# Attention scores of one core: a three-part fp32r product becomes one fp32 product

## The reference, cut to what matters

```python
q = (x @ Wq + bq)                      # 8 heads of 128
kv = x @ Wkv + bkv                     # one key and one value head, shared by the 8
k, v = kv[..., :128], kv[..., 128:]
q = q + pe[None, None, :, :]           # sinusoidal positions
k = k + pe[None, :, :]
scores = einsum('bhqd,bkd->bhqk', q, k) / sqrt(128)
scores = where(causal, scores, min)
attn = einsum('bhqk,bkd->bhqd', softmax(scores), v)
out = attn.reshape(B, T, 8 * 128) @ Wo
```

## Time and profile before

| | us |
|---|---|
| median of 3 runs (lowest to highest) | 880.68 (879.22 to 882.73) |
| the profiled execution's own time | 883.31 |
| its span, first to last instruction | 881.5 |
| PE busy | 680.0 (77%) |
| DVE busy | 546.7 (62%) |
| ACT busy | 415.1 (47%) |
| POOL busy | 300.3 (34%) |

### The profile page before, as it was taken

The page is one execution under the profiler, slowest core; times in us unless marked ns, Lnnn a source line. Parts: engine busy times, 40 slices in busy tenths (PEclk is TensorE's granted clock), DMA queues, the critical chain, the costliest instruction groups (busy, mean ns, idle before and its releaser), DMA issues. The chain is left out here.

```text
span 881.5 us, 11690 instructions
## 1 busy us (share of the span) xinstructions
PE 680.0 (77%) x3456; PEld 474.4 (54%) x3468; DVE 546.7 (62%) x820; ACT 415.1 (47%) x824; POOL 300.3 (34%) x211
## 2 busy tenths in 40 slices
PE   4889999999989689999999898501766666675764
PEld 2656666666659566666666654100555555561222
DVE  5264333343323234433445448977999998999998
ACT  1255555555525355455555668422454552553330
POOL 0012122101100022112211100786776763768882
PEclk9589999999979999999999998855699997996998
DMA  9200000000556500000000000113254552440112
GB/s 306 60 3 10 10 9 12 6 3 7 152 156 214 164 10 10 10 9 9 6 3 7 6 1 1 45 39 119 65 153 147 177 156 83 157 142 24 36 33 57
DMA packets 45761, 57.63 MB, mean 65 GB/s; under 512 B 6049, under 2 KB 32418, under 8 KB 45730
## 3 DMA queue, kind: packets, MB, share of 16 engines
q1 hardware_dynamic: 32994, 46.23, 16.8%
q0 software_dynamic: 3072, 6.30, 2.4%
q10 hardware_dynamic: 9664, 4.72, 1.8%
HBM read 43.60 MB, written 13.63 MB: 65 GB/s over the span
## 5 line engine op out<-in xcount | busy, mean ns | idle before, releaser
L437 POOL TENSOR_TENSOR QL<-QF,QH 128x512 fp32r<-128x512 f32 x32 | 40.6, 1268 | 409.4 <-ACT QH L558 409.4
L1353 DVE TENSOR_REDUCE nmax<-PS 128x1 f32<-128x128 f32 (+7 forms) x128 | 96.6, 756 | 116.2 <-PE PS L828 114.7
L566 ACT COPY PT<-PS 128x512 f32<-128x512 f32 (+1 forms) x192 | 85.8, 482 | 139.0 <-PE PS L840 138.9
L856 PE MATMUL PS<-PT,V 128*128 128x512 f32 (+3 forms) x384 | 151.0, 505 | 0.2 <-ACT PT L566 0.2
L482 POOL TENSOR_TENSOR YA<-YA,HC 128x1024 f32<-128x1024 f32 x44 | 103.9, 2362 | 53.9 <-DVE HS L1514 53.3
L815 PE MATMUL PS<-KH,QH 128*128 128x512 f32 (+1 forms) x192 | 87.3, 455 | 19.6 <-POOL QL L437 19.0
L573 ACT ACTIVATE PR<-PS,nmax 128x128 f32<-128x128 f32 (+7 forms) x128 | 96.4, 753 | 5.5 <-DVE nmax L1353 5.5
L840 PE MATMUL PS<-CST,PR 128*128 128x128 f32 x576 | 85.7, 276 | 14.5 <-ACT PR L573 14.4
L840 PEld LDWEIGHTS PS<-CST,PR 128*128 128x128 f32 x576 | 68.4, 142 | 48.7 <-issue 32.1
L1047 PE MATMUL PS<-R,pickb 128*128 128x512 bf16 x58 | 23.0, 482 | 79.8 <-DVE HS L1514 34.7
L1369 DVE SCALAR_TENSOR_TENSOR X<-PS,rinv,X 128x128 f32<-128x128 f32 x128 | 36.1, 345 | 74.1 <-PE PS L878 74.1
(11 more groups left out here) (200 smaller groups left out, 1287.0 us busy)
## 6 DMA issues: line engine op xcount, KB each, us to landing
mw<-in_w SPq DMA_DIRECT2D x40, 512.0 KB, 4.4
mw<-in_w SPq DMA_DIRECT2D x16, 321.0 KB, 4.1
more_w<-in_w SPq DMA_DIRECT2D x16, 321.0 KB, 3.6
rows_in<-zero SPq DMA_DIRECT2D x18, 256.0 KB, 3.5
MX<-rows_in SPq DMA_DIRECT2D x20, 128.0 KB, 4.2
rows_out<-MY ACTq DMA_DIRECT2D x20, 128.0 KB, 2.8
rows_out<-MY ACTq DMA_DIRECT2D x8, 256.0 KB, 4.3
X<-in_x SPq DMA_DIRECT2D x4, 256.0 KB, 4.2
```

The source lines that it names most:

```text
L566: nc.scalar.copy(dst, src).then_inc(s_ed, 1)
L856: r = mm(PS[:, 6, lo:BANK], V[:, b * TB + j, :], PT[b][:, 4 * group + j, lo:BANK], start=j == 0, stop=True, skip_group_check=True)
L1353: nc.vector.tensor_reduce(nmax[:, i % 4:i % 4 + 1], sc[:, 0:(i + 1) * P], AX_X, ALU.max, negate=True).then_inc(s_nm, 1)
```

## The change

Query and key stay plain fp32 (`Q`, `K`), DVE writes them in place, and the score product is one fp32 matmul. The three-part product, the staging tile `QF`, ACT's `query_high` and its copy to `KH`, GpSimd's `query_low`, DVE's subtraction into `KL`, and the semaphores `s_qh`, `s_qe`, `s_kh` are gone. PE waits for `s_qr`, DVE's signal, where it waited for GpSimd's. The indirect DMAs of GpSimd stand as before, without the `query_low` calls between them.

```diff
-            KH, KL = sb1("KH", [P, B, T], F32R), sb1("KL", [P, B, T], F32R)
+            K = sb1("K", [P, B, T])
-            QH, QL = sb1("QH", [P, T], F32R), sb1("QL", [P, T], F32R)
-            QF = sb1("QF", [P, BANK])
+            Q = sb1("Q", [P, T])
...
# GpSimd
-            def query_low(g, hf):
-
-                pool.wait_ge(s_qh, 2 * g + hf + 1)
-                sl = slice(hf * BANK, (hf + 1) * BANK)
-                nc.gpsimd.tensor_tensor(QL[:, sl], QF[:], QH[:, sl].bitcast(F32), ALU.subtract).then_inc(s_qe, 1)
...
# ScalarE
-                    act.wait_ge(s_kf, 2 * q + 2)
-                    nc.scalar.copy(KH[:, b, (q % 2) * BANK:(q % 2 + 1) * BANK], QF[:]).then_inc(s_kh, 1)
-            def query_high(g, hf):
-                act.wait_ge(s_qr, 2 * g + hf + 1)
-                nc.scalar.copy(QH[:, hf * BANK:(hf + 1) * BANK], QF[:]).then_inc(s_qh, 1)
...
# TensorE
-                        pe.wait_ge(s_kf, 5)
+                        pe.wait_ge(s_kf, 3)
...
-            def three(dst, a, b_, ra, rb, first):
-
-                mm(dst, a[0][ra], b_[0][rb], start=first, stop=False, skip_group_check=True)
-                mm(dst, a[0][ra], b_[1][rb], start=False, stop=False, skip_group_check=True)
-                return mm(dst, a[1][ra], b_[0][rb], start=False, stop=True, skip_group_check=True)
...
-                    three(PS[:, s + lo // BANK, 0:hi - lo], (QH, QL), (KH, KL), q, (slice(None), b, slice(lo, hi)), True)
+                    mm(PS[:, s + lo // BANK, 0:hi - lo], Q[:, i * P:(i + 1) * P], K[:, b, lo:hi], start=True, stop=False,
+                       skip_group_check=True)
...
-                pe.wait_ge(s_qe, 2 * g + 1)
+                pe.wait_ge(s_qr, 2 * g + 1)
                 for i in range(8):
...
                     if i == 4:
-                        pe.wait_ge(s_qe, 2 * g + 2)
+                        pe.wait_ge(s_qr, 2 * g + 2)
...
# VectorE
-                    stt(QF[:], bank(KEY_BANK[q]), bk[:, 0:1], peT[:, sl], ALU.add, ALU.add).then_inc(s_kf, 1)
-                    dve.wait_ge(s_kf, 2 * q + 1)
-                    ts(QF[:], QF[:], SCALE, None, ALU.mult).then_inc(s_kf, 1)
-                    dve.wait_ge(s_kh, q + 1)
-                    tt(KL[:, b, sl], QF[:], KH[:, b, sl].bitcast(F32), ALU.subtract).then_inc(s_ke, 1)
+                    stt(K[:, b, sl], bank(KEY_BANK[q]), bk[:, 0:1], peT[:, sl], ALU.add, ALU.add).then_inc(s_kf, 1)
+                    dve.wait_ge(s_kf, q + 1)
+                    ts(K[:, b, sl], K[:, b, sl], SCALE, None, ALU.mult).then_inc(s_ke, 1)
...
-                stt(QF[:], bank(7), bq[:, bass.ds(h, 1)], peT[:, hf * BANK:(hf + 1) * BANK], ALU.add,
+                stt(Q[:, hf * BANK:(hf + 1) * BANK], bank(7), bq[:, bass.ds(h, 1)], peT[:, hf * BANK:(hf + 1) * BANK], ALU.add,
                     ALU.add).then_inc(s_qr, 1)
```

More of the change, by code:

```diff
@@ L237, in build @@
         s_qr = sem("query_left_psum")
-        s_qh = sem("query_high_ready")
-        s_qe = sem("query_ready")
         s_kf = sem("key_summed")
-        s_kh = sem("key_high_ready")
         s_qk = sem("scores_ready")
@@ L431, in gather @@
                     in_offset=bass.IndirectOffsetOnAxis(ap=slot[m][:, k, t:t + 1], axis=0)).then_inc(s, 16)
-            def query_low(g, hf):
-                pool.wait_ge(s_qh, 2 * g + hf + 1)
-                sl = slice(hf * BANK, (hf + 1) * BANK)
-                nc.gpsimd.tensor_tensor(QL[:, sl], QF[:], QH[:, sl].bitcast(F32), ALU.subtract).then_inc(s_qe, 1)
             def attention(b):
-                query_low(8 * b, 0)
                 for h in range(HEADS):
-                    query_low(8 * b + h, 1)
                     if b == 0:
@@ L451, in attention @@
                             gather(0, 0, t, GA[:, t, :], s_g0[t // TB])
-                    if h < HEADS - 1:
-                        query_low(8 * b + h + 1, 0)
             attention(0)
@@ L583, in head @@
                         deviation(2)
[L584 to L587, removed]
                     if i == 0 and pending:
@@ L600, in attention @@
                 batch[0] = b
-                query_high(8 * b, 0)
                 head(8 * b, False, True)
@@ L823, in scores @@
                 s = 2 * (i % 2)
-                q = (slice(None), slice(i * P, (i + 1) * P))
                 for lo in range(0, nk, BANK):
                     hi = min(nk, lo + BANK)
-                    three(PS[:, s + lo // BANK, 0:hi - lo], (QH, QL), (KH, KL), q, (slice(None), b, slice(lo, hi)), True)
+                    mm(PS[:, s + lo // BANK, 0:hi - lo], Q[:, i * P:(i + 1) * P], K[:, b, lo:hi], start=True, stop=False,
+                       skip_group_check=True)
                 mm(PS[:, s + i // 4, (i % 4) * P:(i % 4 + 1) * P], identb[:], causalb[:], start=False, stop=True,
@@ L1323, in keys_values @@
                     dve.wait_ge(s_wat, 16 * 6)
-                else:
-                    dve.wait_ge(s_qe, 2 * HEADS)
                 for q in (2 * b, 2 * b + 1):
@@ L1328, in keys_values, with q_evac @@
                     sl = slice((q % 2) * BANK, (q % 2 + 1) * BANK)
-                    if q:
-                        dve.wait_ge(s_ke, q)
-                    stt(QF[:], bank(KEY_BANK[q]), bk[:, 0:1], peT[:, sl], ALU.add, ALU.add).then_inc(s_kf, 1)
-                    dve.wait_ge(s_kf, 2 * q + 1)
-                    ts(QF[:], QF[:], SCALE, None, ALU.mult).then_inc(s_kf, 1)
-                    dve.wait_ge(s_kh, q + 1)
-                    tt(KL[:, b, sl], QF[:], KH[:, b, sl].bitcast(F32), ALU.subtract).then_inc(s_ke, 1)
+                    stt(K[:, b, sl], bank(KEY_BANK[q]), bk[:, 0:1], peT[:, sl], ALU.add, ALU.add).then_inc(s_kf, 1)
+                    dve.wait_ge(s_kf, q + 1)
+                    ts(K[:, b, sl], K[:, b, sl], SCALE, None, ALU.mult).then_inc(s_ke, 1)
             keys_values(0)
-            def q_evac(g, hf, first=False):
+            def q_evac(g, hf):
                 dve.wait_ge(s_qp, 2 * g + hf + 1)
-                if not first:
-                    dve.wait_ge(s_qe, 2 * g + hf)
                 h = g - 8 * batch[0]
-                stt(QF[:], bank(7), bq[:, bass.ds(h, 1)], peT[:, hf * BANK:(hf + 1) * BANK], ALU.add,
+                stt(Q[:, hf * BANK:(hf + 1) * BANK], bank(7), bq[:, bass.ds(h, 1)], peT[:, hf * BANK:(hf + 1) * BANK], ALU.add,
                     ALU.add).then_inc(s_qr, 1)
@@ L1391, in attention_start @@
                 batch[0] = b
-                q_evac(8 * b, 0, b == 0)
+                q_evac(8 * b, 0)
                 head(8 * b, False, True, beside=b == 0 and {0: lambda: route(0), 3: lambda: take_ranks(0),
```

## The result

The changed kernel takes 902.5 us (median of 6 runs, 900.7 to 907.0) against 880.0 for the kernel before beside it (878.2 to 888.6): ratio 1.0246, 95% interval 1.0197 to 1.0294. The forecast was 883.9, range 877.5 to 889.0, so it was wrong by 18.6 us. The profiled execution took 901.72 us (span 899.9), 18.4 above that of before.

The account below looks back on a forecast made before the run. PE was taken to bound attention. Later heads +8.5 us, head 8 -2.6, head 0 -2.0 and experts -0.7 summed to +3.2, forecasting 883.9 us on the median's scale, range 877.5 to 889.

Parts of the forecast that it names:

- At nothing: Effects priced at zero: ACT's copies, POOL's subtractions, its indirect DMAs issued in one go early in each stage, and QF.
- Products: PE's fp32 score products take 0.86 us at 512 columns, 0.43 at 256, 0.22 at 128, costing 1.3 us a head.
- Rivals D and E: D: reduced products cost only their columns, 893 us, chance 0.02; E: fp32 products priced differently, inside the forecast's width.
- Tile 4's wait: PE's wait for QL ahead of tile 4's scores goes wholly, gaining 9.2 us over 14 later heads.
- rival A: Tile 4's wait is replaced by one at turn of tile 3 for ACT's exponential: 893.1 us, chance 0.13.
- Tile 0's: PE's wait for QL at tile 0's scores turns into a longer wait for PR of tile 7: gain zero.
- rival B: Tile 0's wait returns too, since ACT without casts delivers tile 7 earlier: 874.8 us, chance 0.11.
- Openings: First heads of both attention stages start about 2 us earlier: head 8 -2.6 us in all, head 0 -2.0.
- The clock at the second opening: In head 8 more scores lie ahead of the clock's fall to half speed, counted as 0.5 us gained.
- rival C: PE stays at full clock through the second opening, some 2 us come back: 881.9 us, chance 0.18.
- Experts: At the experts' start PE's 1.47 us wait for MXT shortens without the subtraction into KL: -0.7 us.
- one of my cases at 0.28: Slower than can be told from no change: rivals A and D and the forecast's upper quarter, together 0.28.

Follow-up runs that it names:

- e1: The changed kernel with GpSimd's indirect DMAs spread two or three per head by waits, nothing else: 882.8 us, ratio 0.9998 to the kernel before.
- e2: The changed kernel with both runs of 16 indirect DMAs whole, but started only in tile 2 of heads 3 and 11: 904.7 us, 1.0257.
- e10: The changed kernel, 16 indirect DMAs from each stage's start, one 128x16 GpSimd subtraction after every fourth: 901.9 us, 1.0215.
- e9: The changed kernel, 16 indirect DMAs from each stage's start, one 128x16 GpSimd subtraction after each: 883.3 us, 1.0008.
- e7: The changed kernel with plain DMAs of the same 64 KB in place of attention's indirect ones, routing left out: 882.6 us, 0.9998.
- e5: The changed kernel with each stage's indirect DMAs in two runs of eight, at heads 1 and 4 (9 and 12): 891.1 us, 1.0083.
- e8: The changed kernel with each stage's indirect DMAs in runs of four, at heads 1 to 4 (9 to 12): 882.4 us, 0.9999.
- w1: The kernel before with QL subtracted on DVE instead of GpSimd and the indirect DMAs spread as in e1: 873.4 us, ratio 0.9873.
- m1: e1 plus a tail after the stored outputs, ACT and DVE working alone or by turns beside indirect gathers; ACT's copies started late though waiting for nobody.
- m6: e1 plus a tail of PE and DVE turns beside gathers with various GpSimd fillers or none; first three stages and the unfilled run of 16 lost nothing.

## Why the prediction was wrong

- **The step that failed** stands under "At nothing": "POOL's indirect DMAs, no longer held by the subtractions, are issued in one go early in each stage", priced at zero, with "the transfers would meet only `Wq` loads" if the cover failed. I asked when the rows arrive and what the transfers collide with, not what issuing them that fast does to other engines. The runs: 19 to 22 us for 32 DMAs (e1 against the changed kernel and e2, and e10 against e9), nothing at one DMA in 1.4 us. The subtractions that the change removed, each with its wait for ACT's cast, had been the spacing. The Trainium skill, DMA: Bandwidth & Descriptors, Anatomy of one DMA (SWDGE path), says of descriptor generation that "You can emit a lot of descriptors before the incremental cost shows up". For the issuing engine this case agrees (0.94 to 0.98 us each, the sixteenth as the second; the very first took 1.17); the cost showed up on the other engines, in runs of more than four.
- **Products**: right; 0.86, 0.43 and 0.22 us as taken from the earlier trace rows. Rivals D and E are out.
- **Tile 4's wait**: right (by the weight load's rows the 14 waits sum to 8.8 us and not 9.2, the longest being 1.01); it is gone, with no new wait at `turn` of tile 3, so rival A is out. **Tile 0's**: right; the wait for `PR` grew to 1.36 and nothing returned, so rival B is out.
- **Openings**: the second starts 2.1 us sooner behind the query, as said. Head 0 is 1.9 shorter in e1 by its first scores (21.6 against 23.5), but other kernels with the same head 0 have it at 19.4 (e2, e7) to 21.9 (e5, e8, e9) in their traces, so this match is weak.
- **The clock at the second opening**: mis-sized; rival C came, to which I gave 0.18. Where the kernel before had 6.83 us at half clock, the changed kernel has a clock of 1.00 (the row from 312.71 to 320.00 above) and falls only at 327.42, behind PE's idle time; e1 keeps 1.00 through head 8, which takes 16.5 us against 19.3. With the start that is 4.8 us where the sum has 2.6: the 2 us of rival C. In the changed kernel the run of DMAs hid it. The stretch in e1:

```profile
303.71:310.54 6.83, 6.25 (x29) 3.56 (x30) 3.25 (x6) 3.31 (x11) 1.05 (x2) 1.00 0.03 10
```

- **Experts**: mis-sized. PE waited 0.78 for `MXT`, from 1.47, as said. But from the first experts to the query behind them e1 takes 36.75 us and the kernel before 39.89 (261.92 to 301.81): there PE waited 3.6 us for the loads of `more_w`, in e1 1.3 (0.22, 0.55 and 0.52). PE in the kernel before, then in e1:

```profile
290.46 2.02 PE L959 MATMUL PS<-MXT,more_w 128*128 128x128 f32 x16 [1.37 <-DMA more_w<-in_w]
296.92 2.02 PE L959 MATMUL PS<-MXT,more_w 128*128 128x128 f32 x16 [2.20 <-DMA more_w<-in_w]
```

```profile
264.99 3.78 PE L930 MATMUL PS<-MXT,mw 128*128 128x128 f32 x16 [0.78 <-DVE MXT L1377]
...
292.09 2.02 PE L930 MATMUL PS<-MXT,more_w 128*128 128x128 f32 x16 [0.55 <-DMA more_w<-in_w]
296.85 2.02 PE L930 MATMUL PS<-MXT,more_w 128*128 128x128 f32 x16 [0.52 <-DMA more_w<-in_w]
301.74 1.12 PE L784 MATMUL PS<-XNT,wq 128*128 128x512 f32 x2 [0.78 <-DVE MY L1384]
```

  So the loads account for 2.3 of these 3.1 us. The half clock there lasts 13.7 us in the kernel before and 10.2 in e1, which has to do with the rest. In part this is chance of the execution: the same stretch takes 36.8 to 38.9 us in the eleven traces with fp32 scores (e8, whose experts are e1's, has 38.9), and 39.9 and 40.2 in the two with reduced ones.

By its profile e1 took 0.8 us less than the kernel before, and my sum is +3.2. The clock gives 2.2 of these 4.0 us and the experts 3.1; what is left, 1.3 us the other way, is spread over the start and the later heads.

The direction, slower, was one of my cases at 0.28, for other reasons. With the DMAs spread (e1) the forecast was 3 to 4 us too high, by gains that the sum had too small; the miss of 18.6 is the two runs less these gains.

## What to carry to other kernels

When work is taken off an engine that also issues DMAs, read that work as their spacing as well: list what the queue issues back to back once it is gone, and price that against every engine, not only against the transfers. A releaser called "remote" on one core meant here that a signal came late; compare its time with the end of the instruction that gives it. And a chain that stands ahead of the bound engine can be shortened (w1) for more than it brings to buy it off with longer work on that engine.

## What the runs showed of the hardware

- Runs of eight or more indirect DMAs of 128 rows, issued by GpSimd faster than about one in 1.4 us (1.25 to 1.36 us lose, 1.37 to 1.47 don't), delayed engines that executed many instructions meanwhile, once some 60 to 80 of these had gone by: PE's signals by up to 11.4 us (changed kernel), ACT's own copies by up to 1.9 each (m1). The tail m6, at 1.25 to 1.35 us, is an exception that nothing here explains. Sixteen plain DMAs at one in 0.55 us, out in 8.7 us, did no harm.
- Why is open. That the engines run short of instructions, because their supply stands behind the descriptors, would fit the counts, but the trace speaks against it: it has packets that load instructions, and in e2 none of them starts between 94.4 and 187.3 us, around a run that cost as much (whether it records them all isn't known). Another cause that fits the counts and was not tried is the profiler's own recording of each instruction: every execution on record comes with the profiler's span and clock, so no run here rules it out.
- In the changed kernel's first stage it is over some 3 us after the last DMA (78.11 to 81.78). But PE's idle time in it is followed by a lower clock, 0.61 of full speed from 327 to 344 us in the changed kernel, which adds to the loss.
